# The two roundings of each half of the queries, one unit later on ScalarE and VectorE

## The reference, cut to what matters

```
x = layernorm(x + state_space_mixer(x))          # scan over time, sigmoid gate, W_out
x = layernorm(x + cross_attention(x, ctx))       # 16 heads of 16, 64 context rows per batch
x = layernorm(x + mixture_of_experts(x))         # 8 experts, each takes its 256 best tokens

# cross_attention
Q = x @ Wq + bq;  K = ctx @ Wk + bk;  V = ctx @ Wv + bv
attn = softmax(Q K^T / 4);  out = attn V;  return out @ Wo + bo
```

## Time and profile before

| | us |
|---|---|
| median of three runs | 296.37 |
| lowest and highest | 293.88, 305.04 |
| span of the profiled execution, first to last instruction | 301.2 |
| busy: TensorE matmuls / weight loads | 249.7 / 205.1 |
| busy: VectorE / ScalarE / GpSimd | 193.8 / 159.7 / 137.8 |

### The profile page before, as it was taken

How to read it: one execution, slowest core, us unless ns; L and a number is a source line. 1 busy time by engine, 2 the same in 40 slices (tenths; PEclk the granted TensorE clock), 3 DMA queues, 4 the chain that set the end, 5 groups by cost and what they waited for, 6 DMA issues and landing times.

```text
span 301.2 us, 5168 instructions
## 1 busy us (share of the span) xinstructions
PE 249.7 (83%) x1689; PEld 205.1 (68%) x1689; DVE 193.8 (64%) x594; ACT 159.7 (53%) x336; POOL 137.8 (46%) x205
## 2 busy tenths in 40 slices
PE   8999999899988999999997111376599999999990
PEld 4756458575556879989895111336599999999890
DVE  1743357368957478848777788751267866776495
ACT  3654512525587356565324677212357987875454
POOL 6813955626253301555567976077453144443000
PEclk9999999999999799999999555557599999999998
DMA  6960013036192817469000399223226745522665
GB/s 185 291 139 16 1 31 77 0 70 139 32 209 64 181 42 150 114 164 307 4 1 1 111 394 291 86 73 108 71 55 160 204 71 113 125 33 26 159 218 209
DMA packets 33403, 35.59 MB, mean 118 GB/s; under 512 B 10338, under 2 KB 25698, under 8 KB 33122
## 3 DMA queue, kind: packets, MB, share of 16 engines
q1 hardware_dynamic: 29858, 30.90, 36.5%
q0 software_dynamic: 2784, 4.00, 7.8%
q10 hardware_dynamic: 736, 0.38, 0.4%
HBM read 18.16 MB, written 8.19 MB: 87 GB/s over the span
## 4 chain that ended last, share of the span: by engine, by line
PE 58%; DVE 16%; ACT 10%; issue 5%; DMA 4%; POOL 2%; another core or an unknown queue 2%; SPq 1%; DVEq 0%; POOLq 0%; ACTq 0%
PE bank L1218 13%; PE bank L1464 9%; PE bank L1675 6%; PE bank L1415 4%; DVE junk L2042 3%; PE bank L1307 3%; PE bank L1383 2%; PE bank L1451 2%; DMA Y<-summed_rows 2%; PE bank L1398 2%; ACT bank L1135 2%; PE bank L1427 1%; PE bank L1228 1%; DMA summed_rows<-OUT,idx 1%
## 5 line engine op out<-in xcount | busy, mean ns | idle before, releaser
L881 POOL DMA_INDIRECT summed_rows<-OUT,idx x14 | 21.8, 1556 | 37.8 <-DVE OUT L2160 35.7
L807 POOL TENSOR_SCALAR var_eps<-mean_var 128x1 f32<-128x1 f32 x32 | 7.3, 227 | 59.4 <-DVE mean_var L1886 59.0
L1464 PEld LDWEIGHTS bank<-VB,PT 128*128 128x128 f32 x256 | 33.0, 194 | 1.6
L1464 PE MATMUL bank<-VB,PT 128*128 128x34 f32 x256 | 31.4, 270 | 0.0
L1135 ACT ACTIVATE bank<-bank,b_up_c 128x256 f32<-128x256 f32 (+1 forms) x48 | 19.5, 447 | 18.1 <-PE bank L1218 13.0
L1218 PE MATMUL bank<-FTH,WUH 128*128 128x256 f32 x94 | 28.4, 302 | 0.0
L1218 PE MATMUL bank<-FTL,WUH 128*128 128x256 f32 x94 | 27.6, 293 | 0.0
L1218 PE MATMUL bank<-FTH,WUL 128*128 128x256 f32 x94 | 27.6, 293 | 0.0
L1893 DVE TENSOR_REDUCE NMF<-bank 128x8 f32<-128x512 f32 x32 | 21.7, 681 | 8.1 <-PE bank L1427 8.0
L1675 PE MATMUL bank<-WDH,MH 128*128 128x256 f32 x80 | 23.2, 290 | 1.2 <-DVE ML L2174 1.2
L871 POOL DMA_INDIRECT XG<-routed_rows,idx x16 | 15.5, 971 | 18.1 <-DVE idx L2136 13.8
(11 more groups left out here) (350 smaller groups left out, 743.4 us busy)
## 6 DMA issues: line engine op xcount, KB each, us to landing
WDR<-in_L_ffn_W_down SPq DMA_DIRECT2D x8, 640.0 KB
QS<-QH SPq DMA_DIRECT2D x32, 128.0 KB, 3.0
WUR<-in_L_ffn_W_up SPq DMA_DIRECT2D x4, 682.0 KB, 4.8
routed_rows<-X SPq DMA_DIRECT2D x2, 1056.0 KB, 10.0
X<-in_x SPq DMA_DIRECT2D x4, 512.0 KB, 5.1
QS<-QL SPq DMA_DIRECT2D x16, 128.0 KB, 3.0
summed_rows<-X SPq DMA_DIRECT2D x2, 1024.0 KB, 6.0
Y<-summed_rows SPq DMA_DIRECT2D x8, 256.0 KB, 5.5
```

The costliest lines, as they stand in the source:

```text
L881: pool.indirect_dma_start(summed, bass.IndirectOffsetOnAxis(ap=idx[:, 2 * e + h:2 * e + h + 1].bitcast(U32), axis=0), OUT[:, (2 * e + h) % ...
L1464: last = pe.matmul(o[:, j * 34:(j + 1) * 34], PT[m % 2][:, j, s * P:(s + 1) * P], VB[:, m // 2, j].rearrange("p h d -> p (h d)"), start=Tr ...
```

## The change

For half c of block n, QH on ScalarE and QL on VectorE move from unit 4n + c to unit 4n + c + 1. Within the unit they stand further ahead than before: QH right behind the first normalisation, ahead of gates and exponentials; QL behind the statistics of z1, ahead of the second reduction of the maxima. The instructions, their operands and the semaphores that they wait for and raise are the same. TensorE's, GpSimd's and SP's lists are unchanged.

```
 ScalarE
                 if live(g - 1, "z1"):
                     normalise(1, g - 1 - LAG["z1"])
+                for c in range(KC):
+                    n = block_of(g - 1 - c, "q")
+                    if n is not None:
+                        wait_filled(act, ("q", n, c))
+                        if n >= 2:
+                            wait_filled(act, ("mx", TPB * (n - 1) - 1, KC - 1))
+                            act.wait_ge(qs_in[n % 2], 16 * 3 * 4 * (n // 2))
+                        act.activation(QH[:, n % 2, c], bank_of(("q", n, c))[:], ACT.Identity,
+                                       bias=bq_c[:, c:c + 1]).then_inc(q_hi, 1)
                 for q in GATE_UNITS.get(g, ()):
                     gate_out(q)
...
-                for c in range(KC):
-                    n = block_of(g - c, "q")
-                    (the same body)
                 if live(g, "att"):
 VectorE
                 if live(g, "z1"):
                     statistics(1, z1, ("z1", z1))
+                for c in range(KC):
+                    n = block_of(g - 1 - c, "q")
+                    if n is not None:
+                        dve.wait_ge(q_hi, KC * n + c + 1)
+                        dve.scalar_tensor_tensor(QL[:, n % 2, c], bank_of(("q", n, c))[:], bq_c[:, c:c + 1],
+                                                 QH[:, n % 2, c].bitcast(F32), ALU.add, ALU.subtract)\
+                            .then_inc(sem_moved(("q", n, c)), 1)
                 if live(g, "mx"):
                     maxima(mx, 1)
...
                 if live(g, "pv"):
                     attended(pv)
-                for c in range(KC):
-                    n = block_of(g - c, "q")
-                    (the same body)
                 if live(g, "att"):
```

## The result

The changed kernel takes 300.19 us in the median of four runs (299.25 to 302.0), the kernel before 295.38 in the median of four. The ratio is **1.0173, 95% interval 1.0112 to 1.0234**: slower by 5.1 us of 295 (the interval is 3.3 to 6.9 us), where 5.3 were forecast. Some executions are longer as a whole (305.04 us among the four of the kernel before; by its span, the traced one of before too), and the ratios here leave them out.

What follows compares the result with a forecast made beforehand. The prediction took TensorE to hold most of the chain of waits, with a loop of all engines from 75 to 97 us. Delays of 5.9 us less 0.6 gave +5.3 on 296.4, so 301.7 us, range 296 to 308.

Steps and rivals of the forecast that it cites:

- Block 0, half 0: Unit 1: TensorE's product of half 1 must wait for QL to read bank 1, moving TensorE by 2.0 us.
- Block 0, half 1: Unit 2: QL ahead of the second reduction delays the aggregate by 0.66 us more, 2.66 in total.
- Block 1: Units 5 and 6: product of half 1 waits 2.1 us more, total 4.8; QL then adds 0.15, total 4.95.
- Block 2: Units 9 and 10: product 1.4 us later, beside QH delaying the exponentials by 0.95 us; total 5.9.
- Block 3: Units 13 and 14: QL costs nothing, and the transposed maxima's 0.59 us wait for ATL goes; -0.6 us.
- SP's queue: Query DMAs of blocks 0 and 1 start later, but their readers stand five units on; costed at nothing.
- The clock: TensorE's clock fall kept as before in the sum; bounds from -1.7 us (fall gone) to +3.4 (two more).
- a fall of the clock more: Rival: after the stall in unit 1 or 5, dense work runs at half clock; one fall 303.4 us; chance 0.22.
- The stalls are absorbed: Rival: TensorE catches up its hold-ups in units 1 and 5; about 2.2 us in all, 298.6 us; chance 0.18.
- Faster: Rival: VectorE, freed of waits, adds early in blocks 1 and 2, ATL earlier; 1.6 us won, 294.8; chance 0.10.

Runs made afterwards that it cites:

- bank0: The changed kernel with the queries of block 0, half 1, put into PSUM bank 0 instead of bank 1; ratio 1.0104 to the kernel before.
- half1: The kernel before with QH and QL of half 1 alone one unit later, half 0 as before; ratio 1.0066.
- best: Kernel before with block 3 as in the change and, in blocks 0-2, only QL of half 1 later, behind the maxima's low part; ratio 0.9968.
- control: The kernel before, run and traced again without any edit; 296.2 us in whole.
- fill: The kernel before with four unused products of 512 columns put into TensorE's list ahead of unit 11; ratio 0.9996.
- half0: The kernel before with QH and QL of half 0 alone one unit later, half 1 as before; ratio 1.0171.
- last_only: The kernel before with only block 3 as in the change, blocks 0 to 2 as before; ratio 0.9983.
- qh_only: The kernel before with QH alone moved to its new place, QL at its old one; ratio 1.0399.

## Why the prediction was right

The forecast was 301.7 us and +5.3. Measured were 300.19 us, 0.0173 x 295 = +5.1, and in the stage, without the clock's fall, 117.80 - 112.59 = **+5.21 us**. The total is 1.5 us below the forecast, 1.0 of it because the base was taken as 296.37, from three runs, and is 295.38 in four. Step by step:

- *Block 0, half 0* (+2.0): product 8.41 against 6.48, +1.93. bank0 shows the cause, half1 the absence.
- *Block 0, half 1* (0.66 more, 2.66): transposes 17.29 against 14.60, +2.69; half1 alone has 0.66.
- *Block 1* (4.8, then 4.95): 26.05 - 21.29 = +4.76, then 33.64 - 28.66 = +4.98. In the change QL's 0.66 us is nearly paid by the adding that comes early; best, where QL leaves the place altogether, gains 0.5 instead.
- *Block 2* (1.4, of which 0.95 counts, total 5.9): the product +6.48, the transposes +5.97. The 1.5 us of the product lay beside the wait for ScalarE's copy, as supposed: that wait went from 0.99 to 0.41 us. The path behind it moved by 0.99 more. That the term of 0.95 fits so well is in part luck: the exponential moved from 93.28 to 99.08, 5.80 us, which is only 0.8 more than the path ahead of it, since ScalarE's instructions start 0.50 and 0.61 us after one another and the prediction added their whole 0.60 and 0.69.
- *Block 3* (-0.6): from product 3/0 to the maxima 7.86 instead of 8.59, -0.73. QL after the first reduction cost nothing; the wait of 0.59 us went, and a little more.
- *SP's queue* (nothing): no wait of the scores for the query copies appears in the changed kernel, only 0.2 us of one weight load for the copy of the maxima (1.1 before).
- *The clock*: the sum left the fall of before as it was. In the changed trace it had gone, which is the lower end (-1.7) that the bounds kept. The 1.7 us was the author's estimate, the clock missing in three windows of the earlier trace rows, 1.5 x (0.26 + 0.50 + 0.38); no run shows that term. In its place the traces show 1.44 to 1.49 us, from the two with the fall (control, before) to fill without it, at the products of block 3. A direct comparison of the traces before and after gives only 117.80 - 114.08 = +3.7 in the stage. The ratio's interval of 3.3 to 6.9 us holds both 3.7 and 5.2, so the whole time alone does not confirm the sum; the stage does. Of the four runs of the changed kernel two have a mean clock of 0.933 and 299.3 us, two 0.926 and 301.5 us. The rival "a fall of the clock more" may be what separates them, but no such run was traced, and fill's trace shows that a mean clock of 0.923 needs no fall in the stage.

*The stalls are absorbed* failed: half0 alone is +5.15. *Faster* failed at the point that was named for it: QL of half 0 is not out before TensorE needs the bank. The prediction also weighed how idle TensorE is ahead of a fall, and the runs do not show that this decides: before fell to 0.50 behind a stretch with TensorE busy 0.51 of 1.50 us, last_only kept 1.00 behind the same 0.51.

## What to carry to other kernels

Idle time of an engine before an instruction is no gain waiting to be collected: ask which buffer that instruction clears, who takes it next, and how late it may come. Here VectorE's 11.0 us of waiting were nearly free (best has 5.4 of them left and gained 1.24), and moving the instruction out of them cost 5 us on the engine that takes the bank. Move the uses one at a time. Of eight, two were better late (block 3): the bank was not wanted sooner, and what shares another bank, ATH and ATL, went ahead of them. Three (half 1) could go behind the low part of the maxima, where one gained 0.5 us and two cost nothing. Three (half 0 of blocks 0 to 2) were best where they were.

And compare stages, not spans: the slower kernel had the shorter profile (297.5 us to 301.2).

## What was not expected of the hardware

TensorE's granted clock is not fixed by the order of work at this grain: of before and last_only, which do the same up to block 3, one fell and one did not. More idle time did not bring a fall either. The changed kernel kept 1.00 through these stretches,

```profile
77.50:79.00 1.50, 0.54 (x3) 1.00 0.02 3
79.00:80.50 1.50, 0.57 (x2) 1.00 0.00 0
...
94.50:96.00 1.50, 0.19 (x2) 1.00 0.56 127
```

while the kernel before fell to 0.50 behind one of 0.51 of 1.50 us, and qh_only stayed there for some 13 us though TensorE was busy 1.50 of 1.50. The fall of before cost 1.44 to 1.49 us in the middle of the stage. What decides between executions was not settled.
